# Two layers of cross-attention: VectorE's and ScalarE's order of work in the first block of the second pass

## The reference

```python
# layer 0: 16 heads of 64, masked, softmax over the 128 keys
qh, kh, vh = x @ Wq + bq, ctx @ Wk + bk, ctx @ Wv + bv
a = exp((qh @ kh.T) * mask - max) * mask
out = (a / (sum(a) + 1e-15)) @ vh
x1 = layernorm(out @ Wo + bo + x) * gamma + beta
# layer 1: 16 heads of 32, no mask
q, k, v = x1 @ Wq1.T, ctx @ Wk1.T, ctx @ Wv1.T
out = softmax(q @ k.T / sqrt(32)) @ v
y = layernorm(x1 + out @ Wo1.T + bo1) * gamma1 + beta1
```

## Time and profile before

| | |
|---|---|
| device time, median of 3 runs | 836.01 us (835.39 to 836.18) |
| device time of the profiled execution | 838.48 us |
| its span, first to last instruction | 836.5 us |
| TensorE, share of the span | 98% |
| VectorE / ScalarE / GpSimd | 66% / 54% / 57% |
| mean granted TensorE clock | 0.996 |

### The profile page before, as it was taken

One profiled execution on the slowest core, in us unless ns is written; L12 is line 12 of the kernel. 1 busy time (PEld: TensorE's weight loads), 2 busy tenths in 40 slices (PEclk: granted clock), 3 DMA queues, 4 the chain that ended last, 5 costly groups with the idle time before them and its releaser, 6 DMA issues.

```text
span 836.5 us, 12619 instructions
## 1 busy us (share of the span) xinstructions
PE 818.0 (98%) x4564; PEld 553.5 (66%) x4564; DVE 554.9 (66%) x1278; ACT 454.9 (54%) x575; POOL 478.5 (57%) x311
## 2 busy tenths in 40 slices
PE   8999999999999999998999999999999999999996
PEld 6777475756666575475668677587686775876744
DVE  3568676667676676866764855756648557567577
ACT  4415363736455554726474673864755738647262
POOL 2022404031231403355889989899889898996636
PEclk9999999999999999999999999999999999999999
DMA  9508534251617053799192461562623714612002
GB/s 305 216 24 299 192 131 179 89 217 51 232 42 259 18 203 103 237 334 248 46 220 67 136 193 39 142 174 73 197 72 126 202 38 139 176 51 76 1 26 76
DMA packets 73661, 118.13 MB, mean 141 GB/s; under 512 B 27776, under 2 KB 34176, under 8 KB 73600
## 3 DMA queue, kind: packets, MB, share of 16 engines
q1 hardware_dynamic: 72640, 117.00, 44.6%
q10 hardware_dynamic: 960, 0.34, 0.2%
HBM read 77.47 MB, written 34.08 MB: 133 GB/s over the span
## 4 chain that ended last, share of the span: by engine, by line
PE 83%; DMA 5%; DVE 3%; SPq 3%; issue 2%; POOL 2%; ACT 2%; DVEq 0%; POOLq 0%; ACTq 0%
PE bank L545 19%; PE bank L547 18%; PE bank L546 18%; PE bank L607 6%; PE bank L577 6%; PE bank L584 6%; PE bank L747 3%; PE bank L766 3%; DMA wk_sb<-wk 1%; DMA sums_dram<-sums_out 1%; DVE scores L1397 1%; DMA r_dram<-den 1%; DMA u_dram<-u_out 1%; PE bank L533 1%; DMA r_bc<-r_dram 1%
## 5 line engine op out<-in xcount | busy, mean ns | idle before, releaser
L1639 POOL TENSOR_TENSOR x_lo<-x_raw,x_hi 128x2048 fp32r<-128x2048 f32 (+1 forms) x8 | 35.6, 4450 | 196.5 <-ACT x_hi L930 180.8
L545 PE MATMUL bank<-wo_lo,a_hi 128*128 128x512 f32 x320 | 127.7, 399 | 1.5 <-DVE z L1371 1.5
L546 PE MATMUL bank<-wo_hi,a_lo 128*128 128x512 f32 x320 | 124.7, 390 | 0.0
L547 PE MATMUL bank<-wo_hi,a_hi 128*128 128x512 f32 x320 | 124.7, 390 | 0.0
L1248 DVE CUSTOM_DVE_ANT_0 scores<-bank,mask_f 128x512 f32<-128x512 f32 x128 | 80.9, 687 | 51.9 <-PE bank L577 51.9
L1681 POOL TENSOR_TENSOR a_lo<-a_raw,a_hi 128x1024 fp32r<-128x1024 f32 x32 | 78.0, 2438 | 45.3 <-ACT a_hi L1025 44.5
L545 PE MATMUL bank<-x_lo,wq_hi 128*128 128x512 f32 x256 | 101.2, 395 | 0.6 <-DVE q_lo L1237 0.6
L546 PE MATMUL bank<-x_hi,wq_lo 128*128 128x512 f32 x256 | 99.8, 390 | 0.0
L547 PE MATMUL bank<-x_hi,wq_hi 128*128 128x512 f32 x256 | 99.7, 390 | 0.0
L942 ACT ACTIVATE q_hi<-bank,bq_sb 128x512 fp32r<-128x512 f32 x64 | 44.1, 690 | 101.1 <-PE bank L547 97.9
L1070 ACT ACTIVATE scores<-scores,sh 128x512 f32<-128x512 f32 x128 | 80.2, 711 | 25.1 <-DVE sh L1422 25.0
(11 more groups left out here) (183 smaller groups left out, 1732.7 us busy)
## 6 DMA issues: line engine op xcount, KB each, us to landing
u_dram<-u_out SPq DMA_DIRECT2D x8, 2048.0 KB, 7.6
a_raw<-u_dram SPq DMA_DIRECT2D x32, 512.0 KB, 4.2
r_bc<-r_dram SPq DMA_DIRECT2D x56, 256.0 KB, 5.0
x_raw<-x_t SPq DMA_DIRECT2D x8, 1024.0 KB, 5.6
xn<-x_n SPq DMA_DIRECT2D x8, 1024.0 KB, 5.3
xb_dram<-xn SPq DMA_DIRECT2D x8, 1024.0 KB, 6.0
z<-xb_dram SPq DMA_DIRECT2D x32, 256.0 KB, 2.8
out<-z SPq DMA_DIRECT2D x6, 1024.0 KB, 4.8
```

The costliest lines, as they stand in the source:

```text
L545: nc.tensor.matmul(dst, lh, rl, start=first, stop=False)
L546: nc.tensor.matmul(dst, ll, rh, start=False, stop=False)
L547: return nc.tensor.matmul(dst, lh, rh, start=False, stop=last)
```

## The change

Only block 0 of the second pass is touched. On VectorE, `rows0(0, 1)` and `rows0(0, 2)` with their statistics go ahead of `divisors0(2, 3, 4, 5)` and its reciprocal, which now stand behind `wq1_low(3)`; `divisors0(6, 7)` goes behind the copies of layer 1's values. The first two `wq1_low` stand behind `rows0(0, 2)`. On ScalarE, `normal0(0, 2)` goes ahead of the two joins. On GpSimd, `yt_low(0, 0)` goes between `scales0` of tile 2 and of tile 3.

```diff
@@ ScalarE, second pass, block i @@
+                if not before:
+                    normal0(i, 2)
                 join(i, 0)
                 yt_high(i, 0)
                 join(i, 1)
                 yt_high(i, 1)
-                normal0(i, 2)
+                if before:
+                    normal0(i, 2)
@@ VectorE @@
                 moments0(i, 0)
-                if not before:
-                    divisors0(2, 3, 4, 5)
-                    factors0(slice(0, P), slice(1, 3), 4, 6)
                 rows0(i, 1)
                 statistics0(i, 1)
                 moments0(i, 1)
-                if i == 0:
-                    wq1_low(0)
-                    wq1_low(1)
...
                 rows0(i, 2)
                 statistics0(i, 2)
                 moments0(i, 2)
+                if i == 0:
+                    wq1_low(0)
+                    wq1_low(1)
                 rows0(i, 3)
                 statistics0(i, 3)
                 moments0(i, 3)
                 if i == 0:
                     wq1_low(2)
                     wq1_low(3)
-                    divisors0(6, 7)
-                    factors0(slice(0, P), 3, 2, NB)
+                    divisors0(2, 3, 4, 5)
+                    factors0(slice(0, P), slice(1, 3), 4, 6)
...
                     v1_copy(0)
                     v1_copy(1)
+                    divisors0(6, 7)
+                    factors0(slice(0, P), 3, 2, NB)
@@ GpSimd @@
                     scales0(i, 2, 3)
+                    yt_low(i, 0)
                     scales0(i, 3, 4)
-                    for n in (0, 1):
-                        yt_low(i, n)
+                    yt_low(i, 1)
```

## The result

The changed kernel takes **841.89 us** (median of 4 runs, 840.75 to 843.96); the kernel before, beside it, 836.1 us (4 runs, 835.39 to 836.72). The ratio is **1.0072**, 95% interval 1.005 to 1.0095: slower by 5.8 us, where no change was forecast and 838.0 was the range's upper end. The profiled execution took 843.96 us with a span of 842.2.

The account below looks back on a forecast made before the run. TensorE, busy 98% of the span, bounds the kernel, but another chain fixes the first logits; 0 for waits, -0.1 for the chain and 0 for queues gave -0.1 us, 835.9 us, range 834.0 to 838.0.

Parts of the forecast that it names:

- 383.7 foretold: TensorE's product of the values in block 0: its end at 383.7, where it had been 385.32.
- foretold 388.3: Tile 3 ready for turning on TensorE: between 387.2 and 389.6, taken as 388.3, against 388.5 before.
- the signs that were named for being wrong: r_bc landing over 1 us from 390.0, a clock row under 1 before 396, or 404 to 408 at full clock.
- The argument from the earlier trace: logits1(0, 0) starts at 396.86 and logits1(0, 1) at 402.03, however early TensorE gets there.
- The turned tile: Turning DMA on SyncE: issued at 377.8 instead of 378.88, landing at 382.1, with 383.1 as the other end.
- The sum: 0 for the 4.1 us of waits, -0.1 for the chain, 0 for the queues: -0.1 us, 835.9 us.
- The rival's mechanism: TensorE's clock falls in one longer stop, 384.3 to about 388.5: +2 us, 838.0; chance 0.11.
- Those of 6 and 7 … take at most 4.1 us … Hidden, with 0.4 us to spare by that bound.: VectorE's divisors behind the value copies: from about 391.5 to 395.6 at latest, before q1_low(0, 0) at 396.0.
- Nothing in this chain waits for an operation that the change moves.: Chain from the sums over store_r(1), spread divisors, GpSimd, ScalarE and VectorE to the first logits: untouched by the change.
- I take nothing; the other end is 0.5 us: SyncE's load_u(1, 2) goes 4 to 6 us later, at 395 to 397; cost 0, at most 0.5 us.

Follow-up runs that it names:

- e1: Changed kernel with divisors0(6, 7) and its reciprocal directly behind divisors0(2, 3, 4, 5): 836.92 us, ratio 1.0.
- e7: Changed kernel, normal0(0, 3) also ahead of joins, divisors 2 to 5 before wq1_low(0), 6 and 7 behind wq1_low(3), both tiles scaled before yt_low: 837.59 us, ratio 1.0012.
- e3: Kernel before with only ScalarE's and GpSimd's parts of the change: 836.0 us, ratio 0.9993.
- e9: Changed kernel with the two additions for tiles 6 and 7 done by ScalarE, reciprocals left on VectorE: 837.34 us, ratio 1.001.
- e2: Changed kernel with ScalarE's and GpSimd's parts undone, only VectorE's new order left: 843.02 us, ratio 1.0061.
- e4: Kernel before with only divisors0(6, 7) and its reciprocal moved behind the value copies: 842.86 us, ratio 1.0055.
- e5: Changed kernel with den laid over spread_even, so wo1_lo waits for no store of r: 842.54 us, ratio 1.0067.
- e6: Changed kernel with the two additions of divisors0(6, 7) as tensor_tensor instead of tensor_scalar: 841.31 us, ratio 1.0049.
- e10: Changed kernel with SyncE's loads of u and r for the next half of heads ahead of the stores of tiles 6 and 7: 842.41 us, ratio 1.007.
- e11: Changed kernel with den laid over spread_even and SyncE's next u and r loads ahead of the stores of tiles 6 and 7: 837.07 us, ratio 1.0006.
- e12: Kernel before plus ScalarE's and GpSimd's parts, query parts before wo1_hi, wo1_lo behind first scores, one attention0 on VectorE, resid_scale moved within GpSimd: 838.56 us, ratio 1.0027.

## Why the prediction was wrong

*Right.* The change does to TensorE's waits what was said. The stop of 1.51 us is gone; `output0(0, 3)` and the values end earlier (383.27, against 383.7 foretold), tile 2 is turned at once, then TensorE stops for tile 3, until 388.73 (foretold 388.3). One of the signs that were named for being wrong came as well: a clock row under 1 before 396. And the waits won are worth nothing: e1, which keeps them, is at 1.0 (0.9983 to 1.0018). The argument from the earlier trace rows, that `logits1(0, 0)` hangs on r, GpSimd, ScalarE and VectorE and not on TensorE, stands where the additions are early (e1, e7); in the changed kernel the chain goes over TensorE's values and the copy to the additions.

*The turned tile.* It came at 383.05 (382.1 was taken, 383.1 was the other end), though SyncE issued it at 376.30 and not at 377.8: 6.7 us from issue to landing, and 4.27 before. In both kernels SyncE's wait for the store ahead of it, `store_r(1)`, ends just before, at 382.8 and 382.9. The rule of the Trainium skill, "DMA: Bandwidth & Descriptors", section "Queues, rings and completion order", agrees with this time. The sum did not hang on it.

*The clock.* The rival's mechanism came: it fell in a stop of 4.85 us, and the last four matmuls of the values took 3.62 us, which took 1.88 in the kernel before. Its price was wrong where VectorE's two additions do not stand behind the values: e1, e3 and e9 have a fall and lose nothing. But it has a part in the loss. In all six traces with stretched additions (the changed kernel, e2, e4, e5, e6, e10) the clock had fallen before the second value copy, and the copy ended 4.0 to 4.5 us behind the start of GpSimd's first product. GpSimd is idle from 2.4 to 3.5 us behind it, so the copy's end, and with it the additions, fell into `a_lo`. In e11 the clock stayed up, the copy ended at 3.0 us, and the additions passed. No run holds the clock up by design with the additions behind the copies, so whether the loss needs the fall is not shown. That the clock adds to the loss once the chain is late is seen behind 407 us, where `logits1(0, 2)` loses a further 1.05 us beyond the 4.6; how much of this is the clock's was not measured by itself.

**The first step that failed: "Those of 6 and 7 … take at most 4.1 us … Hidden, with 0.4 us to spare by that bound."** The divisors began 2.4 us later than foretold and took longer than the bound. The value copy ended at 393.95 and not near 391.5, because tile 3 was turned 0.8 us later than before and the last matmuls of the values ran at the low clock, 1.7 us longer. Then additions and reciprocal took 4.30 + 0.95 = 5.25 us. Together this put `q1_low(0, 0)` at 399.14 and not at 396.0. The bound of 4.1 us was that of four additions with their reciprocal in another place. The price of an addition depends on what GpSimd does at that moment, and the earlier trace rows held a hint: two took 1.68 us with an instruction of GpSimd beside them, and four took 2.35, where four take 1.22 in the changed kernel with GpSimd idle. In e1 they take 0.25 each. From 391.5 the additions would have met GpSimd's gap, which lies from 392.15 to 393.31 in this trace (an estimate from its rows); from 393.87 they met `a_lo`.

**The second: "Nothing in this chain waits for an operation that the change moves."** `wo1_lo` writes over the memory of the row sums and therefore waits for all eight stores of r. Before, the stores were long over, and the wait showed in no row. It is in the code, as a wait of VectorE on `r_stored` just ahead of `wo1_lo`. The move of divisors 6 and 7 made it the last to end: 1.87 us, and `wo1_lo` 5 us late.

**The third: "I take nothing; the other end is 0.5 us"** for SyncE. The loads of u went at 400.38, not at 395 to 397, and GpSimd waited 5.51 us. In the changed kernel this lies beside the second and adds nothing clear to it; e5 shows that it costs as much as soon as that one is gone.

The sum of -0.1 us thus lacked one term, the late divisors. By the medians it is 842.86 - 836.42 = 6.4 us with that move alone (e4), and 5.8 us in the whole change. A margin of 0.4 us was called hidden on a bound from another neighbourhood, with the fall of the clock priced apart from the divisors, which it delays.

## What to carry to other kernels

Before a small operation is moved, ask what its new neighbours on the other engines are: an addition of 0.25 us cost some 2.1 us because GpSimd was in the middle of a long instruction, and no row of its old place could say so. List every waiter on the moved result from the code as well, memory reused behind it among them, since a wait that is satisfied early is in no trace. And a wait of the busiest engine is worth only what the chain that it meets next allows: here the stops were removed, moved or lengthened in e1, e3 and e7, and none of it counted. Risks that are priced one by one can also act together: the low clock cost nothing alone, and ahead of the late additions it may have set when they met GpSimd.

## What the runs showed of the hardware that was not expected

A small VectorE addition in SBUF beside GpSimd does not slow down in proportion; in these traces it waits out GpSimd's whole instruction: 1.94 and 2.34 us for one of 0.25 to 0.3, each ending 0.1 us behind GpSimd's. The reciprocal, which has one input, took 0.94 us in e9 with GpSimd's `a_lo` beside it (390.15 to 392.55), the same as alone (0.95 in the changed kernel, where GpSimd is idle). The Trainium skill, "SBUF — State Buffer", section "Who interferes with whom", says that the port pair which the two share is an exclusive lock, and that whoever issues first gets it for the whole instruction. By the same section an operation of a tensor and a scalar can take the pair in its two-port modes, and a VectorE instruction with two SBUF inputs contends with a GpSimd instruction that reads SBUF. Both forms of the addition agree with it here (4.30 us for two, 4.35 in e6), and so does e9, where ScalarE adds two in 0.81 us. It also goes the other way: GpSimd's product took 4.47 us beside `wo1_lo` in e12, against 2.40.

The length of a stop alone did not decide whether the clock fell. It stayed at 1.00 through a stop of 2.61 us in the kernel before, of 2.76 in e11 and of 3.23 in e7; it fell with one of 2.45 us in e9 (0.86 from 386 to 388 us, then 0.50), of 2.57 in e4, of 2.75 in e12, of 3.28 in e3 and 4.85 in the changed kernel. The falls ahead of 394 us in e1, e3 and e9 cost no time that their medians show.
